# Scan stage of a two-layer block on eight cores: the third dequantisation unit of each step moved ahead of the scan

## What is computed

```
xn = layernorm(x)
x  = x + attention(xn) + base_linear(xn) + lora_of_top2_experts(xn)      # layer 0
xn = layernorm(x)
# layer 1, first part: a gated linear recurrence over the tokens
z  = rmsnorm(xn)
a  = sigmoid(A z);  b = B z;  c = silu(Ca z) * (Cb z);  d = sigmoid(D z)
h[t] = a[t] * h[t-1] + (d*b)[t]
y  = c * h
# layer 1, second part: a gated MLP whose weights are stored as 4-bit codes
w_gu, w_down = dequant_fp4(...)           # 11264 x 2048 and 2048 x 5632
x  = x + (Out y + out_b + xn) + rms(w_down (silu(gate(xn)) * up(xn)))
```

## Time and profile before

| | us |
|---|---|
| the two timed runs | 7571.59 and 7998.71, median 7785.15 |
| the profiled execution, its own time | 7554.63 |
| its span on the slowest core (core 6) | 7553.1 |
| spans of the eight cores | 7527.6 to 7553.1 |
| scan stage on core 6, first to last matmul | 3360.9 to 5020 |
| DVE busy between 3360 and 5060 us | 832.7 |
| PE busy between 3360 and 5060 us | 1149.3 |

### The profile page before, as it was taken

The page is one execution under the profiler, slowest core; times in us unless marked ns, Lnnn a source line. Parts: engine busy times, 40 slices in busy tenths (PEclk is TensorE's granted clock), DMA queues, the critical chain, the costliest instruction groups (busy, mean ns, idle before and its releaser), DMA issues.

```text
span 7553.1 us, 64302 instructions; the slowest of 8 cores (7527.6 to 7553.1 us)
## 1 busy us (share of the span) xinstructions
PE 5008.5 (66%) x22156; PEld 2198.5 (29%) x22156; DVE 3149.3 (42%) x5660; ACT 921.1 (12%) x1210; POOL 331.8 (4%) x441
## 2 busy tenths in 40 slices
PE   0365655656563797026776667649888888888886
PEld 0122222222221343002332233224333333333332
DVE  5666666666667201664445544443100110110101
ACT  2022222222221000100000000000000100001000
POOL 0000000000000010001011101101000000000000
PEclk9687877878786898558888888879999999999998
DMA  5321121212112364362333323439543554544643
GB/s 125 100 48 46 43 56 43 51 43 52 47 43 50 62 112 109 96 140 45 55 58 60 58 44 58 63 114 221 154 127 127 154 158 130 152 143 131 162 139 118
DMA packets 936911, 705.39 MB, mean 93 GB/s; under 512 B 288032, under 2 KB 855904, under 8 KB 936592
## 3 DMA queue, kind: packets, MB, share of 16 engines
q1 hardware_dynamic: 578176, 455.66, 19.5%
q0 software_dynamic: 319248, 128.15, 13.9%
q10 hardware_dynamic: 39168, 117.46, 5.3%
HBM read 640.91 MB, written 136.31 MB: 103 GB/s over the span
## 4 chain that ended last, share of the span: by engine, by line
PE 55%; DVE 30%; DMA 6%; issue 6%; ACT 2%; DVEq 1%; SPq 0%; ACTq 0%; POOL 0%; POOLq 0%
PE p_big L1045 12%; PE p_m L1278 8%; PE p_big L1300 8%; PE p_m L1284 8%; PE p_st L535 5%; DVE dq_t L273 4%; DVE dq_t L270 4%; DVE dq_out L277 3%; PE p_big L763 3%; PE p_big L769 3%; DVE RD L668 3%; PE p_big L1163 3%; DVE dq_t L275 2%; DMA XB<-xT 2%; DVE dq_t L268 2%
## 5 line engine op out<-in xcount | busy, mean ns | idle before, releaser
L1045 PE MATMUL p_big<-XN,WM 128*128 128x512 bf16 x5120 | 1149.3, 389 | 739.0 <-ACT CAc L1067 509.8
L1045 PEld LDWEIGHTS p_big<-XN,WM 128*128 128x128 bf16 x5120 | 509.4, 100 | 1379.4 <-issue 803.9
L535 PE MATMUL p_st<-XN,WQH 128*128 128x512 bf16 x3072 | 760.1, 403 | 133.5 <-DVE XN L494 120.7
L589 PE MATMUL p_m<-EB,ONESB 128*128 128x512 bf16 (+3 forms) x640 | 257.1, 405 | 863.6 <-DVE EB L664 772.2
L1278 PE MATMUL p_m<-XN,WG 128*128 128x512 bf16 x2816 | 642.3, 381 | 183.1 <-DVE HQ L1370 163.8
L1300 PE MATMUL p_big<-HQ,WD 128*128 128x512 bf16 x2816 | 635.8, 390 | 74.0 <-ACT SQ L1336 68.9
L1284 PE MATMUL p_m<-XN,WGU 128*128 128x512 bf16 x2816 | 636.5, 379 | 0.0
L1370 DVE SCALAR_TENSOR_TENSOR HQ<-p_m,SG 128x512 bf16<-128x512 f32 x176 | 121.8, 692 | 1231.1 <-PE p_m L1284 1231.1
L535 PEld LDWEIGHTS p_st<-XN,WQH 128*128 128x128 bf16 x3072 | 314.7, 104 | 553.4 <-issue 250.7
L1278 PEld LDWEIGHTS p_m<-XN,WG 128*128 128x128 bf16 x2816 | 264.9, 98 | 563.1 <-issue 275.3
L1300 PEld LDWEIGHTS p_big<-HQ,WD 128*128 128x128 bf16 x2816 | 280.4, 100 | 429.4 <-issue 115.3
(11 more groups left out here) (157 smaller groups left out, 4191.2 us busy)
## 6 DMA issues: line engine op xcount, KB each, us to landing
WG<-s_wgu SPq DMA_DIRECT2D x176, 512.0 KB, 6.1
WGU<-s_wgu SPq DMA_DIRECT2D x176, 512.0 KB, 6.3
WD<-s_wdn SPq DMA_DIRECT2D x64, 1408.0 KB, 7.4
XB<-xT SPq DMA_DIRECT2D x96, 512.0 KB, 4.2
X1B<-s_x ACTq DMA_DIRECT2D x96, 512.0 KB, 4.4
s_wgu<-dq_out SPq DMA_DIRECT2D x88, 512.0 KB, 2.9
WQH<-wqkv POOLq DMA_DIRECT2D x32, 768.0 KB, 13.4
dq_sc<-gusc POOLq DMA_DIRECT2D x88, 256.0 KB, 4.0
```

Source lines behind the costliest of these rows:

```text
L535: i = t.matmul(p_st[:, 0:512], WQH[hh % 2][:, c * 384 + pi * 128:c * 384 + pi * 128 + 128], XN0[:, c * T + s4 * 512:c * T + (s4 + 1) * 512 ...
L589: t.matmul(p_m2[:, qs:512], ONESB[:], EB[gi % 2][:, kti * 512 + qs:(kti + 1) * 512], start=st, stop=last)
L1045: i = t.matmul(p_big[:, half + s2 * 512:half + (s2 + 1) * 512], WM[w][nn % 2][:, c * 128:(c + 1) * 128], Z[:, c * T + th * TH + s2 * 512:c ...
```

## The change

One call for a unit moves on DVE's stream. In every step of the scan stage all three units now stand between the last `UUc` and the scan, and none is left behind `YB`.

```diff
                     kb.inc(i, "p4v", 1)
-                dq.vec(v, 2)
+                dq.vec(v, 3)
                 v.wait_ge(kb.sem("p4s"), 6 * nn + 4)
                 kb.w(v, "p4v", 4 * nn + 4)
                 i = v.tensor_tensor_scan(HHc[:], AAc[:], UUc[:], 0.0, AL.mult, AL.add)
@@
                 i = v.scalar_tensor_tensor(YB[nn % 2][:], HHc[:], 1.0, CCc[:], AL.mult, AL.mult)
                 kb.inc(i, "p4y", 1)
-                dq.vec(v, 1)
```

## The result

The changed kernel is slower: the ratio of its time to that of the kernel before is 1.041, with an interval of 1.032 to 1.050. The prediction had 7886 / 7554.6 = 1.044.

The account below looks back on a forecast made before the run. A ring through PE, DVE and ACT in the scan stage was taken as the bound, 105.8 us a step. (17.1 + 5.0) x 15 = 331.5, less 0.2, gave 331; 7554.6 + 331 = 7886 us, range 7845 to 8130.

Parts of the forecast that it names:

- The ring: Scan stage loop through PE, DVE and ACT, 105.8 us a step; work ahead of the scan lengthens it one for one.
- Term 1: Third unit on DVE, moved ahead of the scan: 17.1 us a step, ends 16.5 and 17.2.
- the prediction's sentence on the shared port: DVE two-port instructions and GpSimd block each other; without overlap the unit takes 16.5 us and the total is 9 lower.
- Term 2: New gap between units 2 and 3, waiting for packed words: 5.0 us a step, ends 3.89 and 7.3.
- Term 3: What comes back behind `YB`: `CCc` read out at once, at most 0.2 us in the stage; clock cost 0.
- Side (c): DVE's total closes the ring, so order does not matter: step stays 105.8 us, time 7555; chance 0.02.
- (a): Rival: the gap ahead of the third unit is at its high end at every step, 7922 us; chance 0.12.
- (b): Rival: the gap vanishes by overlap or the unit runs at its clean length, 7860 us; chance 0.10.
- The range: Range of the time, 7845 to 8130 us; the likeliest case's own range was 7860 to 7925.
- the term for the scatter of the timed runs: Median of two timed runs 231 us above the profiled execution, so near 8116; upper end set at 8130.

Follow-up runs that it names:

- the last experiments: Units put between the `CCc` and `UUc` read-outs: one there, one ahead of the scan, one behind `YB`, 7276.73 us; two there, one behind `YB`, 6992.80 us.
- The two-buffer run: Changed kernel with two output buffers and packed words fetched one unit ahead, from unit 88 on; cores 4 to 7 median 7766.2 us against 7858.5.
- the fastest kernel: Two units between the `CCc` and `UUc` read-outs, none ahead of the scan, one behind `YB`; 6992.80 us, ratio 0.9245 to the kernel before.

## Why the prediction was right, and where it was wrong

**The ring and what it makes of a unit ahead of the scan: right.** The forecast for the profiled execution was 7886 us, the measured 7885.92. That closeness is luck in part. Core 6 grew by 309 us and the medians of the dies by 314 and 319, where 331 was forecast and 306 was the low end. The slowest core of the changed kernel was core 3, which grew by 349 us, 322 of them in the scan stage and 27 in other stages, of which the prediction says nothing.

**Term 1**, the unit, was taken as 17.1 us. From its start to the scan's, the fifteen third units of the changed kernel on core 3 sum to 260.9 us, 17.4 each, a little above the high end of 17.2; the longest took 18.0. Instructions are stretched while POOL issues the weight loads, as here in the third unit of the step shown above:

```profile
4229.83 1.77 POOL L1021 DMA_DIRECT2D WM<-CawT  x2
...
4236.93 1.79 POOL L1021 DMA_DIRECT2D WM<-BwT  x2
```

```profile
4234.58 0.75 DVE L271 TENSOR_SCALAR dq_t<-dq_t 128x512 int16<-128x512 int16 x1
```

The same instruction takes 0.28 or 0.29 us elsewhere in the unit. Behind 4238.8, with the issuing over, none is stretched, though DMA still moves 174 GB/s from 4239 to 4244; and with the weight loads moved away the unit took 16.6 to 17.0 us. So the excess comes with POOL's issuing, as the prediction's sentence on the shared port had it, and not with the transfers. What the prediction had wrong is the overlap. It put the unit 5 us behind the start of the issues, with "some 4 us" shared as before. By its own terms (issues 1.4 us behind the end of unit 2, a gap of 5.0) it would be 3.6 us, and here it was 2.8 us, with 6.1 shared.

**Term 2**, the gap, was taken as 5.0 us and measured 4.4 (66.1 us in 15, from 3.76 to 7.03). The landing under the weight loads was shorter on average than at the three places that the prediction had picked. The two terms are also tied: the shorter the gap, the more of POOL's issuing falls into the unit. The gap of 7.03 was followed by a unit of 16.8 us, the unit of 18.0 stood behind a gap of 3.8. The two errors nearly cancel: 21.8 measured against 22.1.

**Term 3**, what comes back, was taken as 0.2 us in all. There is more: the runs of 320 matmuls are 71.2 us long on average instead of 71.8, so PE gives back 0.6 us a step, 9 us in the stage. PE's idle grew by 328.7 / 15 = 21.9 us a step, and 21.9 - 0.6 = 21.3 is the growth of the step. The prediction argued that a longer idle can't make the restart slower. It did not; that it became a little quicker has a cause that stays open, see the last section.

**Side (c), not slower**, failed at the point that the prediction named: DVE's idle ahead of `UUc` stayed at 33.31 us, while PE worked. Moving work elsewhere on DVE does not shorten it; only units put into that very place use it, as the last experiments show. **(a)**, the high end of the gap, occurred once (7.03). **(b)** was nearer for the gap than the value taken: nine of the fifteen were under 4 us.

**The range: wrong.** The median of the eleven timed runs is 8257.44 us, above the range's end of 8130. The step that failed is the term for the scatter of the timed runs. The prediction put a median 231 us above the profiled execution ("near 8116") and let the upper end take in "a median with one such upper run". The 231 came from two timed runs of the kernel before: half of their distance (213.6) and the 17 us by which the lower one lay above the profiled execution. Measured, the median lies 8257.44 - 7885.92 = 371.5 us above the profiled execution in the changed kernel, and 8013.33 - 7554.63 = 458.7 us in the kernel before, whose ten runs reach 8323.88. Even the one upper run that the prediction had, moved up by the whole cost, would have asked for 7998.71 + 331 = 8330. Nothing in the mechanism of the change is touched: the medians differ by 244 us and the lowest runs by 7885.92 - 7571.59 = 314.

## What to carry to other kernels

Before moving work on an in-order engine, draw the ring of the loop and ask of each place on that engine what it waits for next and who waits for it: here one unit of 17 us cost 21 us a step when it was added ahead of the scan and nothing behind `YB`. Taken from ahead of the scan and put into the idle ahead of a read-out that waits for TensorE, one unit won 20.5 us a step and two won 36.7. A place that is free for one piece need not be free for two. A handshake through DMA (store, then load) is free only as long as other work of the waiting engine stands between two pieces, so count it (here 3.8 to 7.0 us a time) as part of whatever is placed back to back.

## What the runs showed that was not expected

PE did not always come back to the full clock after the same time, and no run says why. After 34 us of idle in the kernel before, with loads under way at 181 GB/s, the granted clock was 0.57 in the fifth and sixth microsecond. In the changed kernel, after 55 us of idle and with the loads already landed, the windows on core 3 read (length, busy times, then the granted clock, DMA share and GB/s):

```profile
4259.60:4261.60 2.00, 2.00 (x5) 0.69 (x6) 0.00 (x0) 0.77 (x1) 0.00 (x0) 0.50 0.00 0
4261.60:4263.60 2.00, 2.00 (x6) 0.73 (x5) 0.00 (x0) 0.00 (x0) 0.00 (x0) 0.53 0.00 0
4263.60:4265.60 2.00, 2.00 (x12) 0.88 (x10) 0.00 (x0) 0.00 (x0) 0.00 (x0) 1.00 0.00 0
```

Here it is at the full 2.4 GHz about four microseconds into the run. But another restart of the same core, at 4005.57, just as quiet, had only 0.67 in the fifth and sixth microsecond, and its run took 71.84 us, as long as in the kernel before. By the mean of the runs of 320 matmuls it looks as if loads in flight made the restart slower: 71.8 us in the kernel before with loads, 71.2 in the changed one without, 71.7 with the loads moved behind `YB` after 54.6 us of idle. The two-buffer run speaks against that. Its restarts on core 5 are quiet too, after 48 us of idle, and its runs are 71.7 us on average; the fifth and sixth microsecond of one:

```profile
3987.33:3989.33 2.00, 2.00 (x7) 0.73 (x6) 0.00 (x0) 0.00 (x0) 0.00 (x0) 0.69 0.00 0
```

So neither the loads alone nor the length of the idle puts these runs in order, and the cause of the 0.6 us stays open.

In the fastest kernel, with eight cores at work, PE on core 2 was granted the full clock for 1030 us of unbroken matmuls, at 215.9 ns a matmul (69.1 us / 320):

```profile
3440.00:4470.00 1030.00, 1024.72 (x4676) 466.55 (x4770) 793.75 (x1497) 133.28 (x120) 149.81 (x186) 1.00 0.53 84
```
